# A fused attention pair on one NeuronCore: first two iterations merged into one written order, batch 1's scores left to the second, and new orders and banks in the last three

## What is computed

```python
# layer 0: 8 heads of 32 channels over 512 positions, q = k = v
q = xt @ Wq.T
scores = scale * jnp.einsum('bhqd,bhkd->bhqk', qh, qh)
logits = (scores * cmask + (1.0 - cmask) * NEG) * rmask
ctx = jnp.einsum('bhqk,bhkd->bhqd', softmax(logits), qh)
x = x + transpose(ctx @ Wo.T)
# layer 1: 16 heads of 32 channels over the 256 rows
xn = rms_norm(x, g_norm) * (1.0 + scale) + shift       # scale, shift = cond @ W_emb + b_emb
q, k, v = xn @ W_qkv                                   # q and k: RMS norm per head
o = softmax(q @ k.T * d ** -0.5) @ v
x = x + o + o @ W_out
```

## Time and profile before

| | us |
|---|---|
| median of 3 runs | 1313.63 (1311.67 to 1318.56) |
| the profiled execution | 1316.98 |
| its span, first to last instruction | 1315.2 |
| PE busy in the span | 1247.5 |
| DVE, POOL, ACT busy | 1034.5, 773.4, 767.3 |

### The profile page before, as it was taken

One profiled execution on the slowest core, in us unless ns is written; L12 is line 12 of the kernel. 1 busy time (PEld: TensorE's weight loads), 2 busy tenths in 40 slices (PEclk: granted clock), 3 DMA queues, 4 the chain that ended last, 5 costly groups with the idle time before them and its releaser, 6 DMA issues.

```text
span 1315.2 us, 20714 instructions
## 1 busy us (share of the span) xinstructions
PE 1247.5 (95%) x6768; PEld 581.5 (44%) x6768; DVE 1034.5 (79%) x916; ACT 767.3 (58%) x1393; POOL 773.4 (59%) x391
## 2 busy tenths in 40 slices
PE   6979899999999999999999999999999999998877
PEld 4424354544444454444445454444545444443433
DVE  4665778878887887889787888888788888877654
ACT  1525566665656666565657666566666656564514
POOL 0245658476665838575574847566583766647442
PEclk8769899999999999999999999999999999999998
DMA  8322544437253433636354342735444363632332
GB/s 279 98 52 78 113 105 99 108 84 169 82 142 101 112 98 92 150 81 162 94 117 111 91 119 81 170 89 124 110 102 107 91 161 82 147 77 57 83 68 61
DMA packets 77960, 143.01 MB, mean 109 GB/s; under 512 B 21536, under 2 KB 23072, under 8 KB 77856
## 3 DMA queue, kind: packets, MB, share of 16 engines
q1 hardware_dynamic: 69136, 126.17, 39.1%
q10 hardware_dynamic: 8720, 15.51, 3.9%
HBM read 32.02 MB, written 8.39 MB: 31 GB/s over the span
## 4 chain that ended last, share of the span: by engine, by line
PE 80%; POOL 6%; issue 4%; DVE 3%; ACT 3%; SPq 2%; ACTq 1%; DMA 1%; POOLq 0%; DVEq 0%
PE PX L530 25%; PE PS L442 9%; PE PO L469 8%; PE PX L564 7%; PE PS L456 6%; PE PO L491 5%; POOL RQK L1928 5%; PE PM L411 4%; PE PX L508 2%; PE PM L508 2%; PE PO L494 2%; PE PM L420 2%; SPq L2071 1%; PE PM L480 1%; PE PM L548 1%
## 5 line engine op out<-in xcount | busy, mean ns | idle before, releaser
L1040 ACT ACTIVATE E<-PS,KBIAS 128x512 f32<-128x512 f32 x512 | 340.0, 686 | 199.0 <-PE PS L442 151.3
L530 PE MATMUL PX<-WQKV,XNT 128*128 128x512 f32 x768 | 383.9, 603 | 3.1 <-ACT V L1018 1.6
L1539 DVE TENSOR_REDUCE NM<-PM 128x4 f32<-128x2048 f32 x128 | 292.1, 2282 | 79.4 <-PE PM L411 79.4
L1916 POOL TENSOR_TENSOR E<-E 128x1024 f32<-128x1024 f32 x112 | 263.1, 2368 | 120.8 <-PE PO L469 107.6
L442 PE MATMUL PS<-B,A 97*128 97x512 f32 x512 | 288.1, 600 | 6.2 <-ACT E L1040 5.3
L1946 POOL TENSOR_TENSOR KQLO<-E 128x1024 f32<-128x1024 f32 x64 | 151.5, 2368 | 229.3 <-ACT E L1047 227.6
L1928 POOL TENSOR_TENSOR RQK<-RQK,HALF 128x16 f32<-128x16 f32 x64 | 211.1, 3303 | 96.6 <-DVE RQK L1627 96.6
L1047 ACT ACTIVATE E<-PS 128x512 f32<-128x512 f32 x256 | 146.9, 597 | 111.1 <-PE PS L456 110.9
L530 PEld LDWEIGHTS PX<-WQKV,XNT 128*128 128x128 f32 x768 | 136.5, 190 | 103.7 <-issue 89.1
L1546 DVE TENSOR_REDUCE NM<-PM 128x8 f32<-128x2048 f32 x64 | 146.4, 2288 | 37.5 <-PE PM L420 37.4
L442 PEld LDWEIGHTS PS<-B,A 97*128 97x128 f32 x512 | 93.3, 192 | 161.6 <-issue 110.2
(11 more groups left out here) (80 smaller groups left out, 1354.3 us busy)
## 6 DMA issues: line engine op xcount, KB each, us to landing
A<-QHI SPq DMA_DIRECT2D x256, 64.0 KB, 2.0
B<-QHI SPq DMA_DIRECT2D x256, 64.0 KB, 2.0
A<-KQHI SPq DMA_DIRECT2D x128, 128.0 KB, 2.4
B<-KQHI SPq DMA_DIRECT2D x128, 128.0 KB, 2.4
XB<-x SPq DMA_DIRECT2D x16, 512.0 KB, 4.0
A<-QLO SPq DMA_DIRECT2D x128, 64.0 KB, 2.0
B<-QLO SPq DMA_DIRECT2D x128, 64.0 KB, 2.0
X<-x ACTq DMA_DIRECT2D x16, 512.0 KB, 4.9
```

Of the source, the lines that this page charges most:

```text
L530: last = mm(PX[:, :], XNT[:, c, t * P:(t + 1) * P], WQKV[:, c, part * DM:(part + 1) * DM], start=(c == 0), stop=(c == 3))
L1040: fn(E[:, probs(seg, i, g), h, :], PS[n % 2][:, :], ACT.Exp, bias=KBIAS[:, g, b:b + 1], scale=SCALE).then_inc(exp_done, 1)
L1539: v.tensor_reduce(NM0[:, q, :].rearrange("p (h k) -> p h k", k=KB0)[:, :, kb], PM[:, :, :], axis=AX.X, op=ALU.max, negate=True).then_inc(m ...
L1916: g_.tensor_tensor(running(seg, i)[:, heads_, :], running(seg, i)[:, heads_, :], E[:, probs(seg, i, g), heads_, :], ALU.add).then_inc(done, 1)
```

## The change

Iterations 0 and 1 become one written order on each engine (`iterations_0_and_1`, in which `i + 1` is iteration 1; iteration 1 itself does nothing), with batch 1's scores all in its second part. Iterations -1, 15, 16 and 17 get new orders. W_emb gets a place of its own (under B1, free until iteration 1) and comes through SP right behind x; W_o, W_qkv and W_out come through SP inside iteration 0. ACT issues half of batch 0's stacks and, in iteration 16, one of four. For the last batch, projections 1 and 3 go to PM's bank 3, `norm_heads` is DVE's instead of POOL's, and the row of maxima goes in two halves through PO, each with four transfers that ACT issues. A helper `keep_warm` is defined and not called.

The diff, cut to its core. The orders of PE and DVE are left out except for iteration 16:

```diff
 BIG = Order(
...
         16: (
+            (("p0", 0), 1, 0), (("p0", 1), 1, 0), (("w0", 0), 0, 0), (("p1", 0), -1, 0), (("p1", 2), -1, 0),
+            (("w1", 0), -2, 0), (("w1", 1), -2, 0), (("v1", 0), -1, 0), (("v1", 1), -1, 0)),
...
+        def heads_bank(b, k):
+
+            return PM[:, 3, :] if b == NB - 1 and k % 2 else PX[:, :]
...
+            def rows1_half(i, b, j):
+
+                pe.wait_ge(context_taken, CONTEXT_TAKEN.ahead(("n1", j), i))
+                pe.wait_ge(max_done, MAXES.upto(("c", 2 * j + 1), i, QUAD))
+                tp(PO[0:H1, j * P:(j + 1) * P], NM1[:, j * H1:(j + 1) * H1], IDENT[:, :]).then_inc(n1_half[j], 1)
...
             def iteration_16(i):
                 qk(i, 0, 0, 1, 2, 3)
-                values_and_sums1(i - 1, i - 2, 3)
                 qk(i, 1, 0, 1, 2, 3)
                 qk(i, 2, 0, 1, 2, 3)
                 qk(i, 3, 0, 1, 2, 3)
-                out1(i, i - 2, 0, 0, 1)
+                out1(i, i - 2, 0, 0)
+                values_and_sums1(i - 1, i - 2, 3)
+                out1(i, i - 2, 0, 1, 2)
                 heads_rows(i, i - 1, 0)
                 heads_rows(i, i - 1, 1)
...
         @block.scalar
...
+            def rows1_half(i, b, j):
+                act.wait_ge(n1_half[j], 1)
+                if j == 0:
+                    act.wait_ge(row1_in.sem, row1_in.at(b - 1))
+                copy(NMT1[0:H1, j, :], PO[0:H1, j * P:(j + 1) * P]).then_inc(context_taken, 1)
+                act.wait_ge(context_taken, CONTEXT_TAKEN.upto(("n1", j), i))
+                for h in range(QH):
+                    act.dma_start(B1[96:97, h, 2 * j:2 * j + 2, :].rearrange("p c (k t) -> p (c k) t", t=P).bitcast(F32),
+                                  NMT1[h * QH:(h + 1) * QH, j, :].bitcast(F32)).then_inc(row1_half_in[j], 16)
...
             def loads():
-                act.wait_ge(wq_in.sem, 16)
-                act.wait_ge(xin_in.sem, xin_in.at(0))
                 act.dma_start(CT[:, :, :], cond_t).then_inc(ct_in.sem, 16)
-                for dst, src in ((WEMB, w_emb.rearrange("(c p) n -> p c n", p=P)),
-                                 (BEMB[:, :], b_emb_t), (GN[:, :], g_norm_t)):
+                for dst, src in ((BEMB[:, :], b_emb_t), (GN[:, :], g_norm_t)):
                     act.dma_start(dst, src).then_inc(mod_in.sem, 16)
-                for dst, src in ((WO[:, :, :], wo_t.rearrange("(c p) n -> p c n", p=P)),
-                                 (WQKV[:, :, :], w_qkv.rearrange("(c p) n -> p c n", p=P)),
-                                 (WOUT[:, :, :], w_out.rearrange("(c p) n -> p c n", p=P)),
-                                 (GQK[:, 0:1], g_q_t), (GQK[:, 1:2], g_k_t)):
-                    act.dma_start(dst, src).then_inc(weights_in.sem, 16)
+                for dst, src in ((GQK[:, 0:1], g_q_t), (GQK[:, 1:2], g_k_t)):
+                    act.dma_start(dst, src).then_inc(gains_in.sem, 16)
...
         @block.vector
...
+            def norm_heads(i, b, k):
+                t, part = k // 2, k % 2
+                rqk = RQK[:, t, part * H1:(part + 1) * H1]
+                dve.wait_ge(rqk_done.sem, rqk_done.at(b, k + 1))
+                heads = QK[:, t, part * DM:(part + 1) * DM].rearrange("p (h d) -> p h d", d=DH)
+                v.tensor_tensor(heads, heads, rqk.unsqueeze(2).broadcast_to([P, H1, DH]), ALU.mult) \
+                    .then_inc(qn_done.sem, 1)
...
         @block.sync
...
+            def load_modulation():
+                sp.dma_start(WEMB[:, :, :], w_emb.rearrange("(c p) n -> p c n", p=P)).then_inc(mod_in.sem, 16)
+
+            def load_weights():
+
+                sp.wait_ge(row0_in[1].sem, row0_in[1].at(0))
+                sp.dma_start(WO[:, :, :], wo_t.rearrange("(c p) n -> p c n", p=P)).then_inc(wo_in.sem, 16)
+                sp.dma_start(WQKV[:, :, :], w_qkv.rearrange("(c p) n -> p c n", p=P)).then_inc(wqkv_in.sem, 16)
+                sp.dma_start(WOUT[:, :, :], w_out.rearrange("(c p) n -> p c n", p=P)).then_inc(wout_in.sem, 16)
...
             def iteration_before(i):
+                load_modulation()
                 stack0(i + 1, 0, 0)
                 stack0(i + 1, 0, 2)
...
+            def iterations_0_and_1(i):
+                load_mask(i)
+                stack0(i + 1, 0, 0)
+                stack0(i + 1, 0, 2)
+                load_weights()
+                load_mask(i + 1)
+                stack0(i + 1, 0, 1)
+                stack0(i + 1, 0, 3)
+                stack0(i + 1, 1, 1)
+                load_x(i + 2)
...
             def iteration_15(i):
                 load_mask(i)
-                stack1(i, i - 1, 0)
                 stack1(i, i - 1, 3)
                 stack1(i, i - 1, 1)
+                stack1(i, i - 1, 2)
+                stack1(i, i - 1, 0)
                 store(i, i - 2)
-                stack1(i, i - 1, 2)
 
             def iteration_16(i):
+                stack1(i, i - 1, 0)
                 stack1(i, i - 1, 1)
-                stack1(i, i - 1, 0)
-                stack1(i, i - 1, 3)
                 stack1(i, i - 1, 2)
                 store(i, i - 2)
```

More of the change, by code:

```diff
@@ L324, in cond_resid @@
         n1_full = ev("n1_full", 1)
+        n1_half = [sem(f"n1_half{j}") for j in range(2)]
+        row1_half_in = [sem(f"row1_half_in{j}") for j in range(2)]
         row1_in = ev("row1_in", 16)
@@ L365, in _ @@
             mm, tp = nc.tensor.matmul, nc.tensor.transpose
-            def modulation(n):
-                if n == 0:
-                    pe.wait_ge(mod_in.sem, 16 * 3)
-                    pe.wait_ge(ct_in.sem, 16)
-                for c in range(4):
-                    last = mm(PO[:, n * NB:(n + 1) * NB], WEMB[:, c, n * P:(n + 1) * P], CT[:, c, :],
-                              start=(c == 0), stop=(c == 3))
-                if n == 7:
-                    last.then_inc(mod_full.sem, 1)
             def small(key, i):
@@ L382, in small, with modulation, keep_warm @@
                 return PM[:, k, :]
+            def modulation(*ns):
+                pe.wait_ge(mod_in.sem, 16 * 3)
+                pe.wait_ge(ct_in.sem, 16)
+                for n in ns:
+                    for c in range(4):
+                        last = mm(PO[:, n * NB:(n + 1) * NB], WEMB[:, c, n * P:(n + 1) * P], CT[:, c, :],
+                                  start=(c == 0), stop=(c == 3))
+                if ns[-1] == 7:
+                    last.then_inc(mod_full.sem, 1)
+            def keep_warm(n):
+                pe.wait_ge(ident_set.sem, 3)
+                for _ in range(n):
+                    mm(PO[:, P:2 * P], IDENT[:, :], IDENT[:, :], start=True, stop=True)
             def quad_free(key, i):
@@ L523, in project1 @@
             def project1(i, key, t, part, full, cs):
+                k = key[1]
+                bank = heads_bank(i - 1, k) if key[0] == "p1" else PX[:, :]
                 if cs[0] == 0:
-                    big(key, i)
+                    if key[0] == "p1" and i == NB and k % 2:
+                        small(key, i)
+                    else:
+                        big(key, i)
+                    if key == ("p1", 0) and i == 1:
+                        pe.wait_ge(wqkv_in.sem, 16)
                     if key == ("p1", 0):
@@ new lines, in iterations_0_and_1 @@
+                exp1(i + 1, i, 2, 1)
+                exp1(i + 1, i, 2, 2)
+                squares(i + 1, i + 1, 1)
+                take_context1(i + 1, i, 0)
+                exp1(i + 1, i, 2, 3)
+                exp1(i + 1, i, 3, 0)
+                exp1(i + 1, i, 3, 1)
+                take_context1(i + 1, i, 1)
+                rows0(i + 1, i + 2, 0)
+                exp1(i + 1, i, 3, 2)
+                norm(i + 1, i + 1)
+                modulate(i + 1, i + 1)
+                exp1(i + 1, i, 3, 3)
@@ L2084, in stack1 @@
                 sp.wait_ge(score_full, SCORES.upto(("C", 15), b))
[L2085 to L2087 removed]
+                for dst, src in stack1_rows(hq):
+                    sp.dma_start(dst, src).then_inc(stack1_in[hq].sem, 16)
             def store(i, b):
```

807 lines of the change are left out of this document (547 added, 260 removed), and 12 rows, old and new, of the table special.

## The result

The changed kernel took **1299.99 us** (median of 4 executions, 1294.54 to 1301.46), the kernel before beside it 1314.93 (4 executions, 1311.67 to 1318.56): ratio 0.9877, 95% interval 0.9854 to 0.9900. Four further executions of the changed kernel gave a median of 1299.66. The forecast was 1301.1. The profiled execution has a span of 1299.3 us instead of 1315.2: 15.9 less, where the medians are 14.9 apart.

A forecast was written before the change was run, and what follows sets the result against it. PE was taken as the bound, busy 95% of the span, with gains only at the ends. Terms -3.0-1.0-5.5-3.0 = -12.5 us, from the 1313.63 median, gave 1301.1 us; range 1292 to 1311.

The forecast's parts named there:

- Start and iteration 0: Kernel start: ACT takes the first projection earlier and the sums of group B come earlier; -3.0 us, bounds +1.0 and -6.5.
- The first chain: At the start: ACT copies the first projection at about 9.6, -3.8 us; one more reduce wait, 2.29 us; transpose about 35.2.
- POOL decides: End of the first iteration: POOL's five adds and one scaling set when the sums of group B come, put at 78.3.
- POOL's floor: Earliest end of POOL's adds and scaling before the sums of group B: 65.1+13.1 = 78.2 us.
- Iteration 1: Second iteration, order rewritten: some PE idle and low clock recovered, mask and stack loads hidden; -1.0 us, bounds +3.0 and -4.0.
- Iteration 15: Mask load after the last power removes PE's 4.0 us wait at sums and 1.7 for stacks; -5.5 us, bounds -2.0 and -6.7.
- The second part of the term: Group C's 1.70 us wait for the stacks goes, because the two stores now come after the last stack.
- Iterations 16 and 17: Tail: two PSUM banks, norm moved to DVE and row in two halves; -3.0 us, bounds -0.6 and -7.0.
- from there the chain is unchanged: Tail: after score (2,0)'s exponential, at 1289.3 to 1289.8 against 1292.95, the rest to the end stays as before.
- (c): Rival: clock stays low through the second iteration, mean granted clock under 0.73; +30 us there, 1332 in all; chance 0.07.
- (a): Rival: the waits move, the ends only exchanging one edge for another; leaves about 5 us, 1308.6; chance 0.22.
- (b): Rival: more than counted, second iteration at full clock and tail keeping the third score's gain; -20 us, 1293.6; chance 0.11.

The follow-up runs named there:

- mask late: Kernel before with one line moved: in iteration 15 POOL's masked_out comes behind the fourth power instead of ahead of the second; 1309.94 us beside 1314.28, ratio 0.9963.

## Why the prediction was right

Right in sign, inside the range, 1.1 us from the median. Part of that is luck. The gain was larger than the forecast -12.5 us, 14.9 in the medians and 15.9 in the spans; the kernel before, measured beside the changed one, lay 1.3 us above the 1313.63 that I subtracted from. Three of the four terms need correction, in both directions.

**Start and iteration 0 (-3.0, measured -4.0, by the means of several traces -6.7).** The first chain was right: ACT's copy at 9.80, one reduce more. The transposes came 1.4 us earlier than the sum said (33.83, not 35.2), since the second projection ran at 2.4 GHz (1.96 us); in four of the six other traces of the same program it took 3.75. The first exponential came at 40.51, not 42: ACT had issued the six transfers of its stack by 38.9, and PE's projection and values (to 40.0) were last; the two were priced as equal. "POOL decides" was wrong: POOL was done at 75.9, and DVE's last add waited 6.07 us for exponentials. The rows of before said so already: that add began at 79.11, a microsecond before POOL ended, and what released it was ACT. POOL's floor was counted from 65.07, but its chain starts with scores that now come earlier (63.05). The weights landed in time, as counted (W_qkv in 13.1 us from 65.92; no wait of PE names it).

**Iteration 1 (-1.0, measured +0.2).** The clock went from 0.92 to 0.97 over the iteration, and PE's idle time grew from 5.65 to 6.79 us (78.03 - 72.38, 78.22 - 71.43). That it can gain shows in the traces with products of the identity at the end of iteration 0 (75.9 us), and once without them: 76.26 us at a clock of 0.99 in the version with the norms on POOL. The other six traces of that program took 78.04 to 78.22.

**Iteration 15 (-5.5, measured -6.5).** The mask and the 4.03 us behind it were right, and shown from both sides. The second part of the term was not: of the 1.70 us for the stacks only 0.5 went, although the stores now stand behind them. The size came out all the same because of two things that the sum left out: the short waits (1.9 us before, 0.95 after, beside the long ones) and 1.0 us that PE's products lost at the lower clock behind the long stand. Over the six traces of the new order in it the mean is 73.05, -5.2: in three of them the wait for the stacks was 1.65 to 2.25 us instead of 1.20 to 1.41, and what followed ran slow (below).

**Iterations 16 and 17 (-3.0, measured -5.4).** The -2.9 of the projections was right in kind and 0.7 too small (13.90 instead of 17.53: -3.6). The maxima came as forecast (-3.35 for -3.2), but for a partly wrong reason: I gave the norm 0.35, and without its move 1.44 of this would have been lost in POOL's queue. The first C scores came 23.4 us behind the last projection, against 25.8 before; I had expected about 20. The exponential of group 2 gained 2.0, not 3.2 to 3.7. The step that failed is "from there the chain is unchanged": from that exponential to the end it took 22.25 us before and 18.9 after. Before, PE was granted 0.84 in 1280 to 1300 us, and a group of value products took 1.94 us in it; now the clock is 1.00 from 1280 us on and each group takes 1.07.

```profile
1298.07 1.94 PE L491 MATMUL PO<-E,V 128*32 128x256 f32 x16
```
```profile
1282.31 1.07 PE L552 MATMUL PO<-E,V 128*32 128x256 f32 x16
```

This part is no single draw: in all twelve traces of the new order the rest took 18.8 to 19.0 us, in the two of the old order 22.25 and 20.95 (mask late, where PE was at the low clock for a shorter time). The chain itself is about as long as it was: its six slow groups of products before lost some 3 us to those at full clock, an estimate from the same groups later in the trace, and 22.25 less that is about 19.2. I had the clock in this stretch only as a loss in the bounds.

**Rivals.** (c) had its condition measured: the clock in iteration 1 is 0.97, far over 0.73. (a) would have needed new waits in iteration 15; the only one over 0.6 us is the old one for the stacks. (b) expected iteration 1 at full clock; in six of seven traces it was at 0.97 and gained nothing. On the rule about POOL's and DVE's shared access to SBUF, which the prediction cites: the norms on DVE took 0.69 us each beside a power, as I had taken, and no cost of 0.7 came; but the powers went from 2.90 to 3.27 and 3.4. Here the one that pays is POOL.

## What to carry to other kernels

Price a moved operation by the whole queue that it leaves: here the norm was worth nothing while projections came each 4.39 us, and 1.44 us once they came each 3.43. An instruction that must wait for a transfer belongs behind the work that others need from the same engine: one moved line was worth 5.4 us. And where PE stands in a start or a tail, ask what clock its next stretch will be granted (a stand of 4.03 us was followed by products at nearly twice their time), and compare several traces before crediting a few microseconds to an edit.

## What the runs showed that I had not expected

The same program starts iteration 1 between 95.91 and 100.67 us, in the order of the clock that PE was granted in 40 to 60 us. In iteration 15 the wait for the stacks differs too. In the version with identity products in three places it was 1.81 us, and followed by four products that took 3.56 us, where the changed kernel needs 1.88:

```profile
1202.85 0.56 PE L527 MATMUL PS<-B,A 97*128 97x256 f32 x2 [1.81 <-DMA B<-KQLO]
1203.20 3.56 PE L608 MATMUL PX<-WQKV,XNT 128*128 128x512 f32 x4
```

With waits of 1.65, 1.81, 2.07 and 2.25 us the iteration took 73.95 to 74.45 us at a mean clock of 0.98; in the seven other traces of this order with the mask late, with waits of 0.50 to 1.56, it took 71.08 to 72.16: some tenths more of waiting went with two microseconds more of iteration. Which comes first, the wait or the lower clock, no run here tells apart. And two engines that are said to lock each other out did so in one case and not in another. The Trainium skill (SBUF — State Buffer, Terms) says that of DVE and GpSimd the loser blocks fully for the other's instruction. Beside an add on POOL the trace of before agrees: the scaling of 0.68 us began 0.43 us behind the add and ended 0.56 behind its end.

```profile
1228.62 2.36 POOL L1946 TENSOR_TENSOR KQLO<-E 128x1024 f32<-128x1024 f32 x1 [9.32 <-ACT E L1047]
1229.05 2.49 DVE L1582 TENSOR_TENSOR QK<-QK,R 128x512 f32<-128x512 f32 x1 [2.34 <-ACT QK L1018]
```

Beside a power it does not hold: with one of 3.27 us on POOL, a norm on DVE still took 0.69, and the power 0.37 us more than alone, about half the norm's time. There the measurement decides. No run here shows what sets the two cases apart.
